# Local attention: q's inverse length as the exponential's scale, the division moved ahead of the transposes

## The reference, cut to what matters

```python
def l2norm(t):
    return t / jnp.clip(jnp.linalg.norm(t, axis=-1, keepdims=True), 1e-12)

qkv = h @ wqkv
q, k, v = jnp.split(qkv, 3, axis=-1)          # then 8 heads of 64
q = l2norm(q) * qs
k = l2norm(k) * ksc
q, k = rotary_xpos(q, k)
# windows of 64 tokens; each sees itself and the window ahead of it
sim = jnp.einsum('bhwid,bhwjd->bhwij', bq, bk)
sim = jnp.where(mask, -jnp.finfo(sim.dtype).max, sim)
attn = jax.nn.softmax(sim, axis=-1)
out = jnp.einsum('bhwij,bhwjd->bhwid', attn, bv)
x = x + o @ wo
```

## Time and profile before

| what | value |
|---|---|
| median of 3 runs | 2242.17 us |
| the profiled execution: time, span | 2243.29 us, 2241.4 us |
| PE, PE weight loads busy | 95%, 66% |
| DVE, ACT, POOL busy | 75%, 69%, 75% |
| instructions | 53938 |
| mean granted PE clock | 0.989 of full speed |

### The profile page before, as it was taken

One profiled execution on the slowest core, in us unless ns is written; L12 is line 12 of the kernel. 1 busy time (PEld: TensorE's weight loads), 2 busy tenths in 40 slices (PEclk: granted clock), 3 DMA queues, 4 the chain that ended last, 5 costly groups with the idle time before them and its releaser, 6 DMA issues.

```text
span 2241.4 us, 53938 instructions
## 1 busy us (share of the span) xinstructions
PE 2125.9 (95%) x19264; PEld 1468.6 (66%) x19264; DVE 1683.1 (75%) x4031; ACT 1541.9 (69%) x4254; POOL 1680.3 (75%) x1712
## 2 busy tenths in 40 slices
PE   6999879999899999899999999999999989999988
PEld 4777557777567777556666656666777756777765
DVE  6777568888568888677677777777888856888865
ACT  3666358888548998626656656657888954889862
POOL 6778779998258888448877787868999834888852
PEclk9999889999999999999999999999999999999999
DMA  4000001112111112121211121111111211111211
GB/s 118 1 1 1 7 21 44 26 41 49 44 32 36 38 39 50 46 67 46 57 46 41 51 58 42 52 27 23 36 32 44 46 45 30 33 38 40 47 31 51
DMA packets 121369, 88.38 MB, mean 39 GB/s; under 512 B 85560, under 2 KB 102160, under 8 KB 118800
## 3 DMA queue, kind: packets, MB, share of 16 engines
q1 hardware_dynamic: 118544, 82.69, 15.3%
q10 hardware_dynamic: 2560, 2.24, 0.4%
HBM read 30.38 MB, written 8.39 MB: 17 GB/s over the span
## 4 chain that ended last, share of the span: by engine, by line
PE 43%; DVE 16%; POOL 14%; issue 5%; SPq 5%; DMA 2%; ACT 1%; POOLq 0%; DVEq 0%
PE bank L1351 11%; POOL store L1163 8%; POOL store L1172 6%; PE bank L1362 5%; PE bank L600 5%; PE bank L1342 5%; DVE store L986 4%; SPq L473 4%; DVE store L991 3%; DVE store L998 3%; PE bank L639 3%; PE bank L730 2%; PE bank L652 2%; PE bank L678 2%; PE bank L614 2%
## 5 line engine op out<-in xcount | busy, mean ns | idle before, releaser
L1575 POOL TENSOR_SCALAR store<-store 128x512 f32<-128x512 f32 x512 | 349.8, 697 | 107.9 <-DVE store L1502 105.9
L1502 DVE CUSTOM_DVE_ANT_0 store<-bank,store 128x512 f32<-128x512 f32 x512 | 335.6, 688 | 120.2 <-PE bank L1342 67.3
L1458 ACT ACTIVATE store<-bank 128x512 f32<-128x512 f32 x512 | 286.8, 600 | 201.5 <-PE bank L1351 198.1
L854 ACT ACTIVATE store<-bank,store 128x128 f32<-128x128 f32 x1024 | 363.4, 375 | 47.9 <-DVE store L1004 47.8
L1163 POOL TENSOR_TENSOR store<-store 128x16 f32<-128x16 f32 x128 | 372.7, 2912 | 27.7 <-DVE store L1000 27.2
L1157 POOL TENSOR_TENSOR store<-store 128x512 f32<-128x512 f32 x256 | 321.2, 1277 | 94.3 <-DVE store L991 90.9
L1351 PEld LDWEIGHTS bank<-store 128*128 128x128 f32 x2048 | 240.1, 142 | 133.5 <-ACT store L1458 75.8
L1351 PE MATMUL bank<-store 128*128 128x128 f32 x2048 | 298.4, 277 | 0.0
L1172 POOL TENSOR_TENSOR store<-store 128x512 f32<-128x512 f32 x256 | 261.7, 1044 | 10.0
L600 PE MATMUL bank<-store 128*128 128x512 f32 x496 | 253.1, 596 | 0.0
L1004 DVE TENSOR_REDUCE store<-bank 128x4 f32<-128x512 f32 x256 | 164.8, 686 | 89.8 <-PE bank L639 89.5
(11 more groups left out here) (224 smaller groups left out, 4556.2 us busy)
## 6 DMA issues: line engine op xcount, KB each, us to landing
store<-store SPq DMA_DIRECT2D x256, 128.0 KB, 2.4
store<-parts SPq DMA_DIRECT2D x96, 192.0 KB
parts<-store SPq DMA_DIRECT2D x16, 384.0 KB, 3.7
store<-store SPq DMA_DIRECT2D x128, 32.0 KB
store<-store SPq DMA_DIRECT2D x128, 31.8 KB
store<-store SPq DMA_DIRECT2D x32, 127.0 KB
store<-in_L_ffn_wqkv_dram SPq DMA_DIRECT2D x4, 768.0 KB, 4.5
out_dram<-store SPq DMA_DIRECT2D x8, 256.0 KB, 2.4
```

What stands on the lines that cost most here:

```text
L854: last = nc.scalar.activation(prob[:, e, b, :], bank[3 + e][:, b * P:(b + 1) * P], ACT.Exp, bias=nmax[:, e, b:b + 1], accum_out=psums[:, h ...
L1458: nc.scalar.activation(AT[:, h % 4, c, :], bank[SCORE_BANKS + (64 * q + 4 * h + c) % TURN_BANKS][:, :], ACT.Exp, scale=-1.0).then_inc(aexp ...
L1502: nc.vector.tensor_tensor_reduce(out=S[:, h % 4, t, :], in0=bank[(64 * q + 4 * h + t) % SCORE_BANKS][:, :], in1=decay[:, off:off + L], sca ...
L1575: nc.gpsimd.tensor_scalar(s_, s_, -1.0, amax[:, h % 4, t:t + 1], ALU.mult, ALU.add).then_inc(shifted_done, 1)
```

## The change

- POOL's power is gone. ACT takes the inverse lengths as Exp(-0.5 Ln(sum of squares)) (`inverse_lengths`, two instructions on 128x16 for a tile), at the end of its turn.
- q is not multiplied by its inverse length: POOL's add of q writes `roped` directly, and the inverse length becomes the `scale` pointer of the exponential. The maximum, taken of the unscaled scores, is multiplied by it first (a 128x4 product on DVE behind each `maxima`).
- The division by the row sums is made on the probabilities ahead of their transposes (`scale_probs`: e=0 on POOL, e=1 on DVE). `weigh_values` now gives the output transposed (values stationary, probabilities moving), so `o_transpose`, `take_o` and `onorm` are gone.
- The transpose, the copy and so on of e=1 move into the next tile's turn, `project_out` and `add_out` into the one after that.
- The mask band is written into the banks by PE for every tile (4 bf16 matmuls); `write_band` on ACT and DVE is gone.
- DVE's clip is a `tensor_tensor` with a constant tile in place of a `tensor_scalar`. Activation tables are loaded ahead of the first `inverse_lengths` of a layer.

The diff, cut to its core:

```diff
+        def inverse_lengths(act, q, j):
+            flat = norm[:, 2 * j:2 * j + 2, :].rearrange("p i h -> p (i h)")
+            act.wait_ge(clip_done, 4 * q + j + 1)
+            nc.scalar.activation(flat, flat, ACT.Ln).then_inc(log_done, 1)
+            act.wait_ge(log_done, 4 * q + j + 1)
+            nc.scalar.activation(flat, flat, ACT.Exp, scale=-0.5).then_inc(norm_done, 1)
...
             def prob_transpose(q, j, e, more):
                 n2 = 8 * q + 2 * j
-                pe.wait_ge(exp_done, n2 + e + 3)
+                pe.wait_ge(scaled_p[e], 4 * q + j + 1)
...
             def weigh_values(q, j):
                 n2 = 8 * q + 2 * j
                 pe.wait_ge(wo_added, 4 * q + j + 1)
                 pe.wait_ge(va_in[j], (32 if j < TPS - 1 else 16) * (q + 1))
-                for e in range(2):
-                    pe.wait_ge(pT_ready, n2 + e + 1)
-                    for b in range(PAIRS):
-                        h = 2 * b + e
-                        for half, v in ((0, VA), (1, V)):
-                            last = nc.tensor.matmul(bank[7][half * WIN:(half + 1) * WIN, h * DH:(h + 1) * DH],
-                                                    probT[:, e, b, half * WIN:(half + 1) * WIN], v[:, j, h * DH:(h + 1) * DH],
+                pe.wait_ge(pT_ready, n2 + 2)
+                for b in range(PAIRS):
+                    for half, v in ((0, VA), (1, V)):
+                        for e in range(2):
+                            h = 2 * b + e
+                            last = nc.tensor.matmul(bank[7][e * DH:(e + 1) * DH, b * P + half * WIN:b * P + (half + 1) * WIN],
+                                                    v[:, j, h * DH:(h + 1) * DH], probT[:, e, b, half * WIN:(half + 1) * WIN],
                                                     start=True, stop=True, skip_group_check=True)
...
-                    scores(q, j, has_prev, ff_ahead and j == 0)
+                    scores(q, j, ff_ahead and j == 0)
                     if has_prev:
-                        weigh_values(*prev)
+                        prob_transpose(*prev, 1, True)
+                    if has_prev2:
+                        project_out(*prev2)
                     if more or j < 2:
                         project_v(*((q, j + 2) if j < 2 else (q + 1, j - 2)), more or j == 0)
                     if has_next:
-                        qk_transpose(*nxt)
+                        if has_prev:
+                            pe.wait_ge(pT_ready, 8 * prev[0] + 2 * prev[1] + 1)
+                        qk_transpose_one(*nxt, 0)
                     if has_prev:
-                        o_transpose(*prev)
-                    prob_transpose(q, j, 0, has_next)
+                        weigh_values(*prev)
+                    if has_next:
+                        qk_transpose_one(*nxt, 1)
                     if has_ahead:
                         project_qk(*ahead, 0)
-                    if has_prev:
-                        project_out(*prev)
-                    if has_ahead:
                         project_qk(*ahead, 1)
-                    prob_transpose(q, j, 1, has_next)
+                    prob_transpose(q, j, 0, has_next)
...
                 for b in range(PAIRS):
-                    h = 2 * b + e
                     last = nc.scalar.activation(prob[:, e, b, :], bank[3 + e][:, b * P:(b + 1) * P], ACT.Exp,
-                                                bias=nmax[:, e, b:b + 1], accum_out=psums[:, h:h + 1])
+                                                bias=nmax[:, e, b:b + 1], scale=norm[:, 2 * j, 2 * b + e:2 * b + e + 1], accum_out=psums[:, e, b:b + 1])
                 last.then_inc(exp_done, 1)
...
             def maxima(q, j, e):
-                dve.wait_ge(sim_done, 8 * q + 2 * j + e + 1)
+                n2 = 8 * q + 2 * j
+                dve.wait_ge(sim_done, n2 + e + 1)
                 nc.vector.tensor_reduce(nmax[:, e, :], bank[3 + e][:, :].rearrange("p (b w) -> p b w", w=P),
-                                        AX.X, ALU.max, negate=True).then_inc(max_done, 1)
+                                        AX.X, ALU.max, negate=True).then_inc(peak_done, 1)
+                if e == 0:
+                    dve.wait_ge(norm_done, 4 * q + j + 1)
+                dve.wait_ge(peak_done, n2 + e + 1)
+                nc.vector.tensor_tensor(nmax[:, e, :], nmax[:, e, :],
+                                        norm[:, 2 * j, :].rearrange("p (b u) -> p u b", u=2)[:, e, :], ALU.mult).then_inc(max_done, 1)
...
+            def scale_probs(q, j, e):
+                dve.wait_ge(pinv_done[e], 4 * q + j + 1)
+                nc.vector.tensor_tensor(prob[:, e, :, :], prob[:, e, :, :], bc(pinv[:, e, :], 2, P), ALU.mult).then_inc(scaled_p[e], 1)
...
+            def scale_probs(q, j):
+                pool.wait_ge(pinv_done[0], 4 * q + j + 1)
+                nc.gpsimd.tensor_tensor(prob[:, 0, :, :], prob[:, 0, :, :], bc(pinv[:, 0, :], 2, P), ALU.mult).then_inc(scaled_p[0], 1)
...
             def finish_qk(q, j):
                 add_turned(q, j, 0)
                 add_turned(q, j, 1)
-                inverse_norms(q, j)
-                normalize(q, j, 0)
-                normalize(q, j, 1)
+                normalize_k(q, j)
```

More of the change, by code:

```diff
@@ L186, in hybrid_block @@
         rope = mem.take(TPS, 2, 2, DH)
-        norm = mem.take(4, H)
+        norm = mem.take(2 * TPS, H)
         qT = mem.take(PAIRS, P)
@@ L817, in transformer_pe @@
                 ff_up(q0, 0, 0, True)
-                o_transpose(q0 + (B - 1), TPS - 1)
                 ff_up(q0, 1, 0, True)
```

158 lines of the change are left out of this document (72 added, 86 removed).

## The result

The changed kernel takes 2288.85 us (median of four runs, 2285.81 to 2289.82), the kernel before beside it 2242.2: a ratio of 1.0206, 95% interval 1.0189 to 1.0224. It is slower, as forecast, and 28 us beyond the 2261 that was forecast, 5 us above the range. The profiled execution is the fastest of the four, 2285.81 us with a span of 2284.0.

A forecast was written before the change was run, and what follows sets the result against it. It took a wait loop through DVE, ACT and PE, 8.56 us a turn, as bound: +18.4 us in the layers, +2.1 at ends, -1.9 at the start, +18.6 on 2243.3, giving 2261 us as median; range 2236 to 2284.

The forecast's parts named there:

- The bound: Attention turns: PE would not be alone; what stands behind a wait in its new order decides, 8.56 us a turn.
- PE's own work: PE's instructions in one attention turn without waits: 8.24 - 0.44 + 0.18 = 7.98 us.
- the first loop: Scores, maximum and product 2.26, exponentials 1.77, copy_pT 0.65, weighing to next scores on PE 3.88: 8.56 us a turn.
- 0.1 us of handoffs either way: Allowance on both loops at 8.56, with 0.07 to 0.11 a pointer: 2248 to 2275 us, chance 0.52.
- 1.4 us less: A layer's first and last turns have less to do: 1.4 us taken off 31 turns of 8.56.
- The ends: Layer ends: later exponentials, reciprocal and division added, take_o and o_transpose gone; +0.5 us each, four times +2.1.
- The start: First layer's start: POOL's power held PE 1.87 us there, so -1.9; the other three starts at nothing.
- The second loop: Through ACT alone: x_transpose waits for copy_v behind both exponential groups and four copies; 8.55 to 8.65 us a turn.
- The scale pointer is free: Exponentials pay nothing for the second pointer; add_out is late next, 8.40 us a turn, 2238 us; chance 0.19.
- PE becomes the bound: PE's work alone sets attention turns, 7.98 us each, 246.0 a layer, 2187 us; chance 0.07.
- The products wait for POOL: DVE's product behind the maximum waits for POOL's k product; with 0.25 us a turn, 2293 us; chance 0.15.
- The rule on the ports: DVE's two-input products and division in store could stand behind POOL instructions, up to 1.04 us more a turn.

The follow-up runs named there:

- the run with both edits: Changed kernel with ACT's copy of the e=1 transposes ahead of the exponentials of e=0 and add_out directly behind the maxima: 2259.0 us, turn 8.34.
- either edit: Changed kernel with the scale pointer left out (2250.5 us), or with ACT's copy of the e=1 transposes ahead of the exponentials of e=0 (2253.3 us).
- the four moves of the last experiments: Changed kernel with copy and add_out moved earlier, copy_v between the exponential groups, copy of o behind those of q and k: 2221.0 us.

## Why the prediction was right in direction and short in size

**The bound, the loop and the sign: right.** The turns are even, POOL's wait before the transposes is gone, PE waits 0.76 us before the weighing (its weight loads 0.97) where 0.5 to 0.7 was forecast, the matmul row names ACT's copy, and the runs with the copy or add_out moved bear the name out: the first took 0.28 off the turn, the second nothing. The pointer costs 0.09 (forecast 0.09). PE's own work is 7.92 (forecast 7.98).

**The step that failed is the sum of the first loop, 8.56.** Measured 8.75, with each part beside its forecast: 2.32 for 2.26, 1.75 for 1.77, 0.74 for 0.65, 3.94 for 3.88. The mechanism is the one named. Two of its handoffs were taken at 0.05 where the turn shows 0.11 (maximum to product) and 0.14 (ACT's copy to a PE that stands): 0.15 of the 0.19. PE's own leg behind the weighing adds 0.06, nearly all of it in the half of the qk_transpose (0.49 for 0.44), and the exponentials take off 0.02. 0.196 by 124 turns is 24.3 us, nearly the whole miss. The "0.1 us of handoffs either way" of the forecast was too little for a loop of several handoffs that runs 124 times.

**The other terms.** The layers' edges add 4.4: their last three intervals are 8.65, 8.33 and 8.85 to 9.50 where PE's idle is longest, and "1.4 us less" was really 0.2 to 0.3. Against it stand 0.8 us by which the third layer was longer than the first already in the kernel before (261.7), which leaves 3.6. The ends were taken at +0.5 each; from last scores to the next layer's first, and to the end of the launch, they measured +1.3, +1.15, +1.75 and +2.55: 4.6 more than forecast. The start came 10.5 earlier in this execution, against 1.9: 8.0 of it is there at the last sum of the block ahead (DVE, 295.0 for 303.0), which the change doesn't touch, and first scores lay between 298.2 and 308.7 in two of the kernels here that share that block. So it is scatter, and it hides a part of the miss: 27.9 (layers) + 4.6 (ends) - 8.6 (start) = 23.9, which is 2285.8 less the 2261.9 forecast for the profiled execution. The other three runs lie 3 to 4 us higher, and the forecast took 1.1 off for the median: that makes the 28.

**The second loop was underpriced too**, 8.55 to 8.65. From the rows of the changed kernel it is 1.75 and 1.73 for the exponentials, 0.48 for the copy between them, 2.10 for the four copies, 0.15 to the transpose of x (the handoff where PE stands for it, in the run with both edits), 0.20 to the band and 2.32 back: 8.73, 0.02 under the first. The run with both edits agrees: its 8.34 lacks the 0.48 and has 0.08 more on the way to its exponentials, which also gives 8.74. The terms that were short are the same kind, handoffs, so the agreement of the two loops could not show the error. By these sums, which are an estimate from the rows, shortening the first loop alone would have gained some 0.02 a turn.

**The rivals.** "The scale pointer is free" was false, but its next loop was right: add_out at 8.40, measured 8.48 with either edit. "PE becomes the bound" needs the four moves of the last experiments; then it is true. "The products wait for POOL": L1010 has a mean of 0.16 us in every run, and the gap is 0.10 for 0.11 where POOL ended 0.48 us ahead of the product (the run with both edits). The tie was there, 0.07 us apart (POOL ends at 2110.74), and no run shows that it cost anything. The rule on the ports held, as the clip and norm_apply show, but off the loop of the changed kernel.

**What the parts are worth.** Power from POOL to ACT in the kernel before -31 us; the pointer in the kernel before +23, in the changed one +38. Order is worth most: four moves of instructions that the changed kernel has anyway (copy, add_out, copy_v, copy of o) took it from 2289 to 2221. The gain of the power's move was real, and was given back twice: by an operand, and by a copy that was queued behind the slowest group of its engine.

## What to carry to other kernels

Where a change puts a copy behind a group of work and another engine's main job behind the copy, write every loop round the engines before judging the parts, and price each handoff by a row in which the receiver stands. Two loops that come out alike mean that an experiment has to shorten one of them alone; here none did. Test the parts alone in the old kernel: here one part took 31 us off, where all of them together added 47. When a test kernel gets a new tile, keep every other tile's place to 64 bytes, and look at where in the launch the time moved before crediting the edit.

## What the runs showed of the hardware

- Tiles moved by 32 bytes: transfers within `store` moved 16 GB/s in place of 18 in their quiet stretches, and 21 us of the launch were lost; moved by 64 bytes, none.
- A DVE 128x16 operation with a constant stands as long behind a running POOL instruction (1.27 us) as one with two inputs. It takes 0.26 where the POOL instruction has 0.22 left, and 0.17 at 283.42 in the changed kernel, where POOL runs nothing.
- The last turn of the fourth layer, with windows of 5 us (busy time by engine, then PE's clock, DMA share, GB/s):

```profile
2187.00:2192.00 5.00, 3.16 (x53) 2.68 (x52) 3.74 (x17) 3.01 (x13) 1.04 (x1) 1.00 0.14 30
2192.00:2197.00 5.00, 4.26 (x57) 3.56 (x61) 2.00 (x7) 4.25 (x13) 2.27 (x3) 0.66 0.00 0
```

PE stood 2.36 us for ACT's copy, and its granted clock in the window behind that was 0.66, a mix of its two levels (1.2 and 2.4 GHz): the weighing took 1.83 us for 1.15, and the interval 9.47. The first and third layer went the same way (0.65 and 0.66). In the second layer PE stood the same 2.36 us, kept 1.00, and the interval was 8.85. So a stall of PE was followed by 0.5 to 0.65 us more in three layers (intervals of 9.36 to 9.50), and by nothing more in the second.
